# Four PSUM banks for the layers of a gated cross-attention block, with x's transposes in borrowed banks

## The reference

```
n   = layernorm(x)
Q,K,V = n @ Wq.T + bq,  ctx @ Wk.T + bk,  ctx @ Wv.T + bv      # per token: 16 heads x 32
p   = softmax over g of  Q[h] . K[g]                            # within one token, heads against heads
a   = sum over g of p[h,g] * V[g]
x   = x + tanh(g_xattn) * (a @ Wo.T + bo)
out = x + tanh(g_ffn) * (layernorm(x) @ (Wf * scale).T + bf)
```

## Time and profile before

| | us |
|---|---|
| median of 3 runs | 311.43 |
| the profiled execution | 311.65 |
| its span, first to last instruction | 309.9 |
| TensorE matmul busy | 276.1 (89%) |
| VectorE busy | 226.8 (73%) |
| ScalarE busy | 127.8 (41%) |
| GpSimd busy | 119.5 (39%) |

### The profile page before, as it was taken

The page is one execution under the profiler, slowest core; times in us unless marked ns, Lnnn a source line. Parts: engine busy times, 40 slices in busy tenths (PEclk is TensorE's granted clock), DMA queues, the critical chain, the costliest instruction groups (busy, mean ns, idle before and its releaser), DMA issues.

```text
span 309.9 us, 7795 instructions
## 1 busy us (share of the span) xinstructions
PE 276.1 (89%) x3124; PEld 220.8 (71%) x3124; DVE 226.8 (73%) x364; ACT 127.8 (41%) x243; POOL 119.5 (39%) x126
## 2 busy tenths in 40 slices
PE   7989995599794599999989999999996999799696
PEld 6868874477673388787868777777775878686585
DVE  3769999569544499579974897489947694698673
ACT  5554344650536202852168204931286006636310
POOL 3143319712255015831382236531583015211732
PEclk9999999689998989999999999999999999899699
DMA  6938881500407640572226530763037102423002
GB/s 229 391 93 268 181 268 71 112 26 0 137 30 242 139 137 4 169 170 98 104 72 203 130 135 0 262 144 135 0 115 184 43 0 70 106 33 122 17 35 102
DMA packets 57830, 37.03 MB, mean 119 GB/s; under 512 B 35920, under 2 KB 45392, under 8 KB 57808
## 3 DMA queue, kind: packets, MB, share of 16 engines
q1 hardware_dynamic: 57808, 36.73, 39.4%
HBM read 25.71 MB, written 11.01 MB: 118 GB/s over the span
## 4 chain that ended last, share of the span: by engine, by line
DVE 25%; DMA 20%; PE 17%; issue 12%; POOL 9%; ACT 8%; SPq 8%; DVEq 0%; POOLq 0%; ACTq 0%
PE acc L463 11%; DMA v_scratch<-v_or_norm 6%; DMA x_scratch<-raw_spare 4%; DMA out<-late 4%; ACT late L775 4%; DVE stats L914 4%; PE score_ps L463 4%; SPq L362 3%; DMA x_spare<-wf_t 3%; POOL rstd L1266 3%; POOL shift L1271 3%; DVE late L1086 2%; DVE spread L1055 2%; DVE k_t L974 2%; SPq L347 2%
## 5 line engine op out<-in xcount | busy, mean ns | idle before, releaser
L463 PE MATMUL acc<-wo_parts,xa_parts 128*128 128x512 f32 x168 | 46.6, 436 | 9.4 <-ACT xa_parts L692 6.8
L1266 POOL TENSOR_TENSOR rstd<-var_eps,minus_half 128x1 f32<-128x1 f32 (+1 forms) x24 | 21.5, 895 | 83.7 <-DVE var_eps L925 83.7
L463 PEld LDWEIGHTS acc<-wo_parts,xa_parts 128*128 128x128 f32 x168 | 34.7, 211 | 18.7 <-issue 4.6
L463 PE MATMUL acc<-wk_parts,ctx_parts 128*128 128x512 f32 x144 | 38.9, 426 | 6.5 <-DVE late L1086 4.1
L775 ACT ACTIVATE late<-attn_ps 32x256 f32<-32x256 f32 x112 | 42.1, 376 | 2.6
L748 ACT ACTIVATE v_or_norm<-late,shift,rstd 128x512 f32<-128x512 f32 x12 | 9.8, 814 | 76.2 <-POOL shift L1271 76.2
L463 PEld LDWEIGHTS acc<-wk_parts,ctx_parts 128*128 128x128 f32 x144 | 28.8, 206 | 15.7 <-issue 5.7
L463 PE MATMUL acc<-wv_parts,ctx_parts 128*128 128x512 f32 x144 | 34.7, 395 | 0.0
L463 PE MATMUL acc<-wq_parts,xa_parts 128*128 128x512 f32 x144 | 33.9, 391 | 0.1
L463 PE MATMUL acc<-wf_parts,x_parts 128*128 128x512 f32 (+1 forms) x132 | 30.1, 383 | 1.9 <-DVE v_or_norm L967 1.9
L463 PEld LDWEIGHTS acc<-wq_parts,xa_parts 128*128 128x128 f32 x144 | 26.7, 188 | 6.2 <-DVE k_t L974 0.4
(11 more groups left out here) (112 smaller groups left out, 465.6 us busy)
## 6 DMA issues: line engine op xcount, KB each, us to landing
x_norm<-x SPq DMA_DIRECT2D x8, 512.0 KB, 3.9
v_scratch<-v_or_norm SPq DMA_DIRECT2D x8, 512.0 KB, 3.2
v_keys<-v_scratch SPq DMA_DIRECT2D x16, 256.0 KB, 3.7
x_res<-x SPq DMA_DIRECT2D x8, 512.0 KB, 3.3
ctx_raw<-ctx_t SPq DMA_DIRECT2D x7, 512.0 KB, 4.5
out<-late SPq DMA_DIRECT2D x13, 256.0 KB, 2.7
x_scratch<-raw_spare SPq DMA_DIRECT2D x5, 512.0 KB, 3.1
raw_spare<-x_scratch SPq DMA_DIRECT2D x20, 128.0 KB, 2.6
```

Of the source, the lines that this page charges most:

```text
L463: last = pe.matmul(dst, left(a, k), right(b, k), start=(n == 0), stop=(n == len(terms) - 1))
L1266: nc.gpsimd.tensor_tensor(rstd[which][:, t], var_eps[which][:, t], minus_half[:, t], ALU.pow).then_inc(n_rstd[which], count)
```

## The change

`turn_ps` is gone and `acc` has four banks: two sets of two. By the function `bank`, v and k write the second set and q, o and f the first, with exceptions: chunk 0's v is in the attention banks, chunk 2 has k and q exchanged, and o of the last two chunks is in the second set. The transposes of x go into score, attention or layer banks for chunks 0, 1 and 2; those of x2 into the score banks, for chunk 5 into layer banks.

```diff
-        acc = [psum(f"acc{i}") for i in range(2)]
-        turn_ps = [psum(f"turn_ps{i}") for i in range(2)]
+        acc = [psum(f"acc{i}") for i in range(2 * TILES)]
...
+        def bank(layer, c, t):
+            even = acc[t][:], acc[TILES + t][:]
+            if layer == "v":
+                return attn_ps[:, BANK * t:BANK * (t + 1)] if first(c) else even[1]
+            if layer == "k":
+                return even[0 if second(c) else 1]
+            if layer == "q":
+                return even[1 if second(c) else 0]
+            if layer == "o":
+                return even[1 if isinstance(c, int) and c >= CHUNKS - 2 else 0]
+            return even[0]
+        def x1_bank(c, t):
+            return (score_ps[t][:], attn_ps[:, BANK * t:BANK * (t + 1)], acc[TILES + t][:])[c]
+        def x2_bank(c, t):
+            return acc[t][:] if late_f(c) else score_ps[t][:]
```

```diff
             def score(c):
...
+                pe.sem_inc(pe_passed, 1)
+                reached(pe, x2_lo, TILES * (c - 2 if final(c) else c - 1))
```

On SyncE, scale and Wf are issued ahead of `load_x(1)`:

```diff
+            sp.dma_start(scale_row[:], scale.partition_broadcast(P)).then_inc(scale_in, DMA)
+            for j in range(2):
+                load_w(WF, j)
             load_x(1)
...
             load_res(0)
-            sp.dma_start(scale_row[:], scale.partition_broadcast(P)).then_inc(scale_in, DMA)
-            for j in range(2):
-                load_w(WF, j)
```

```diff
+            def q_pads(c):
+                act.wait_ge(q_biased, 1 if first(c) else 2)
...
+                for slot in range(PAD):
+                    nc.scalar.activation(q_pad[:, slot], q_t[:], ACT.Identity, scale=own_slot[:, slot:slot + 1]
+                                         ).then_inc(q_padded, 1)
...
             def q_bias(c):
+                dve.wait_ge(q_turned, TILES * (c + 1))
+                nc.vector.tensor_tensor(q_t[:], q_t[:], bq_heads[:].unsqueeze(3).broadcast_to([P, QH, KC, GT]),
+                                        ALU.add).then_inc(q_biased, 1)
```

TensorE's steps after the change:

```diff
             def tensor_step(i):
...
                 score(i)
                 if final(i):
                     o_layer(i - 1, "v", i, (0,))
                     late_f_tile(i - 2, 0)
                     o_layer(i - 1, "v", i, (1,))
+                    attend(i)
+                    turn_x2(i - 1, (0,))
                     late_f_tile(i - 2, 1)
-                    turn_x2(i - 1, x2_read(i - 2), (0,))
-                    attend(i)
                     return
...
+                o_layer(i - 1)
+                k_layer(i + 1)
+                q_layer(i + 1)
                 attend(i)
+                if late_f(i - 1):
+                    v_layer(i + 1, tiles=(0,))
+                    turn_x2(i - 1)
+                    return v_layer(i + 1, tiles=(1,))
+                turn_x2(i - 1)
+                v_layer(i + 1)
+                f_layer(i - 1)
```

```diff
+            def first_step():
                 scores_turn(0)
                 softmax_a(0)
-                q_turn(1, 0)
                 k_bias(1)
-                q_turn(1, 1)
                 softmax_b(0)
                 spread_first(0)
-                q_bias(1)
+                q_turn(1, 0)
+                q_turn(1, 1)
+                dve.wait_ge(bq_made, PAD)
+                q_pads(1)
+                norm_stats(0, x_norm, 2)
                 v_bias(1, 0)
-                norm_stats(0, x_norm, 2)
                 v_bias(1, 1)
...
             def second_step():
...
                 v_bias(2, 0)
-                turned_lo(x2_parts, x2_hi, x2_lo, 0)
+                norm_stats(0, x_norm, 3)
+                x2_low(0)
                 v_bias(2, 1)
-                norm_stats(0, x_norm, 3)
...
             def vector_step(i):
...
                 o_residual(i - 1, 1)
-                turned_lo(xa_parts, x1_hi, x1_lo, i + 1, src=x1_source(i + 1))
+                x1_low(i + 1)
+                if exists(i + 2):
+                    norm_stats(0, x_norm, i + 2)
+                spread_first(i)
+                second_stats(i - 1, 0)
                 k_turn(i + 1, 0)
-                spread_first(i)
+                second_stats(i - 1, 1)
                 k_turn(i + 1, 1)
-                second_stats(i - 1, 0)
                 k_bias(i + 1)
                 q_turn(i + 1, 0)
-                second_stats(i - 1, 1)
-                if exists(i + 2):
-                    norm_stats(0, x_norm, i + 2)
                 q_turn(i + 1, 1)
-                q_bias(i + 1)
-                turned_lo(x2_parts, x2_hi, x2_lo, i - 1)
+                q_pads(i + 1)
...
+                x2_low(i - 1)
```

More of the change, by code:

```diff
@@ new lines, in _ @@
+            exp(0)
+            w_high(WF, 0)
+            w_high(WF, 1)
+            def first_step():
+                spread_some(0)
+                act.wait_ge(gates_done, 1)
+                act.wait_ge(consts_in, 2 * DMA)
+                for row, n in ((bo_row, 0), (bf_row, 1)):
+                    nc.scalar.activation(row[:], row[:], ACT.Identity, scale=tanh_g[:, n:n + 1]
+                                         ).then_inc(rows_scaled, 1)
+                attn_copy(0, (0,))
+                x1_apply(2)
+                attn_copy(0, (1,))
+                x1_high(2)
+                exp(1)
+                attn_copy(0, (2, 3))
+                attn_high(0, 0)
+                attn_high(0, 1)
@@ L1100, in _ @@
             norm_stats(0, x_norm, 0)
+            for t in range(TILES):
+                k_turn(0, t)
             w_low(WV, 1)
             w_low(WQ, 0)
-            turned_lo(xa_parts, x1_hi, x1_lo, 0)
-            for t in range(TILES):
-                k_turn(0, t)
+            x1_low(0)
             w_low(WQ, 1)
@@ L1359, in pool_step @@
                     spread_last(i)
+                if exists(i + 2) and not first(i - 1):
+                    root(0, i + 2)
                 if exists(i - 1):
@@ L1362, in pool_step @@
                     root(1, i - 1, 1, 1)
-                if exists(i + 2):
-                    root(0, i + 2)
+                if first(i - 1):
+                    root(0, 3)
                 if exists(i - 1):
```

411 lines of the change are left out of this document (186 added, 225 removed).

## The result

The kernel after takes 290.13 us (median of 4 runs, 289.82 to 291.31) beside 312.38 us of the kernel before (4 runs); the ratio is 0.937, with a 95% interval from 0.928 to 0.947. Ratios leave out executions more than 1.5% above the fastest of their kernel, so they are not the quotients of the medians. The forecast was 295 us in a range from 287 to 304: the direction and the range held, and the gain was 5 us larger than forecast.

A forecast was written before the change was run, and what follows sets the result against it. TensorE, busy 276.1 of 309.9 us, was taken as the bound, each part priced by its waits. Gains of 4.9 + 4.5 - 2.5 + 2.0 + 7.5 = 16.4 gave a 293.5 us span, forecast 295 us, range 287 to 304.

The forecast's parts named there:

- head, to the queries of chunk 2: Start to chunk 2's query projection: 8.4 us removed, less 3.2 for GpSimd meetings and 0.3 for scalings, gains 4.9 us.
- second step, to the start of the queries of chunk 3: Up to chunk 3's query projection: banks give 1.9 us and an earlier SyncE chain 2.6, together 4.5 (3 to 6).
- low clock behind its stand: TensorE stands some 5 us before chunk 3's queries and its clock falls: 2.5 us lost, ends 1.5 and 3.4.
- middle, score 3 to score 6: Regular middle steps: feed-forward no longer waits for the value bias; gain 2.0 us, ends 0 and 2.7.
- tail, score 6 to the end: Last steps: new orders cover stands and low clock, 10.5 us in all; gain 7.5, 8.5 at best, 2.4 at worst.
- 0.3 for the scalings: Head: ScalarE's scalings replacing padding for chunks 0 and 2 cost 0.3 us; for chunk 0, 0 to at most 0.8.
- Part 2: Stretch to chunk 3's query projection: key stands go, chunk 0's store is late next; 4.5 us gained, 2.5 lost to clock.
- the 1.9 us go: Middle: TensorE's waits for the value bias, 1.9 us in four steps, vanish as feed-forward leaves the value projection's bank.
- The wait of 1.85 stays in part, about 1.1: Tail: of TensorE's 1.85 us wait about 1.1 stays, as ScalarE has chunk 5's x2 between its copies.
- the first rival: Whole kernel: GpSimd costs VectorE nothing and the clock holds, 288 us; chance 0.22.
- The second rival: Second step: head's time is given back at the store if SyncE's chain starts no earlier, 304 us; chance 0.18.
- The third: Later steps: slower, the store stays late in every step and query projections wait, 325 us; chance 0.05.

The follow-up runs named there:

- a run without that wait: Kernel after with chunk 0's store issued ahead of the load of chunk 2's values: 285.17 us, ratio 0.925.
- the run with both edits: Kernel after with statistics of the next x set back late and keys and queries on exchanged banks from chunk 2 on: 296.75 us, ratio 0.951.
- the run with late statistics: Kernel after with statistics of the next x set back behind those of x2 in the regular steps, as before: 297.26 us, ratio 0.954.

## Why the prediction was right, and what it had too small

The sum of terms, each against its measurement from the marks of the two traces:

| term | forecast | measured |
|---|---|---|
| head, to the queries of chunk 2 | 4.9 | 3.7 (64.14 to 60.46) |
| second step, to the start of the queries of chunk 3 | 4.5 | 4.4 (8.05 less 3.7) |
| low clock behind its stand | -2.5 | -2.1 (score 3 is 5.9 earlier, the queries 8.05) |
| middle, score 3 to score 6 | 2.0 | 4.5 |
| tail, score 6 to the end | 7.5 | 10.0 |
| sum | 16.4 | 20.5 |

**Head.** The mechanism held: no stand before chunk 2's transposes, GpSimd's four weight instructions done at 46.3 us (I had said 46), subtraction at 2.23 us, spreading at 2.58. The meetings took 4.6 us of VectorE's time (1.5 + 1.8 + 1.35 against rows without one), near the upper end of 5.6 that I had drawn, and TensorE stood 1.22 and 2.59 us behind them, 3.8 where I took 3.2. The step that failed is "0.3 for the scalings": score 0 came at 33.56, past the 33 us that I had named as a sign of error, since ScalarE's two scalings (2.17 us) ran until 33.26 and TensorE stood 1.15 us for them, past my bound of 0.8. I had costed the edit by ScalarE's duration alone and had not placed it behind the normalization of chunk 1. Another 0.9 us is most likely not the change's: the keys of chunk 1 start at 25.94 against 25.02 in the kernel before, but at 25.84 in the run with the store first in the kernel before, whose edit acts later. That run reaches the queries of chunk 2 at 65.19; against it the head gave 4.7 us, close to the forecast of 4.9, and that nearness is partly luck, as the scalings and the meetings cost more than I took.

**Second step.** The store was late next, as forecast: VectorE stood 5.35 us for it and TensorE 6.10, and a run without that wait took both away. VectorE's residual came 6.2 us earlier (101.19 against 107.42), of which 3.7 are the head's, so the chain itself gave 2.5 where I had 2.6. Part 2 was right in its mechanism. That its 4.5 meets 4.4 so closely is partly luck: the same code stood 4.99 us in another execution and took 7.21 for the queries.

**Middle.** The failing step is "the 1.9 us go" and "ends 0 and 2.7": I added up listed waits. In three steps 4.5 us came. From the start of the value projection to the next scores, where feed-forward's wait of 0.6 us lay, the kernel before took 11.97 us and the kernel after 11.09: 2.6 us in three steps instead of 1.9. From the output projection to the attention, where the keys are, it took 17.27 and 16.54: 2.2 us, against about 0.1 in my sum. I had seen this part as VectorE's 2.2 us of waiting for the store, but left it out of TensorE's sum, whose list shows 0.24 us for it; the keys' row showed it as duration, 6.05 against 5.60. Before x2's transposes 0.2 us were lost. That the keys' part was the store, through the late statistics, is shown by the run with both edits, in which the pattern comes back; neither of the two edits alone brings it back in the keys.

**Tail.** The failing step is "The wait of 1.85 stays in part, about 1.1", and the 1 us taken off beyond that. All the 10.5 us of the earlier trace rows went but 0.5: the waits left from score 6 on are 0.45, 0.33, 0.30, 0.21 and 0.16 us, and the clock stayed at 1.00. TensorE's timeline where the earlier trace rows had the 1.85:

```profile
253.04 1.19 PE L479 MATMUL acc<-wo_parts,xa_parts 128*128 128x512 f32 x4 [0.45 <-ACT xa_parts L709]
254.56 2.11 PE L479 MATMUL acc<-wo_parts,xa_parts 128*128 128x512 f32 x8 [0.33 <-DVE xa_parts L933]
256.51 2.89 PE L479 MATMUL acc<-wf_parts,x_parts 128*128 128x512 f32 x12
```

Setting back the last attention on TensorE costs 2.7 us of it. How the other 7.3 divide between the output projection ahead of the keys, ScalarE's order and the banks I did not separate.

**Rivals.** The measured 290 us lies nearer to the first rival's 288 than to the forecast's 295. Its reason did not hold, though: GpSimd was not free for VectorE, and the granted clock fell to 0.69 behind the stand at 107. The time came near through the middle and the tail, which gave 5 us more than forecast. What spoke for this rival was misread, too. The pair of subtractions at 35.11 did not slip between GpSimd's instructions: one was under way and ended at 35.75, so only 0.64 us of it were left to meet.

```profile
33.35 2.40 POOL L1277 TENSOR_TENSOR ctx_parts<-ctx_raw,ctx_parts 128x1024 fp32r<-128x1024 f32 x1 [6.27 <-ACT ctx_parts L692]
```

Nor was GpSimd quiet at 171.81: its context split ran until 172.07. Beside an idle GpSimd the pair takes 0.75 us (at 40.48 in the kernel before with the early weight) and not 0.87. The second rival fell: the save began at 84.37 in place of 91.50, so the chain did start earlier. The third did not occur, but the run with late statistics shows that its mechanism is real.

## What to carry to other kernels

In this kernel a wait cost more than its row (0.95 us for a listed 0.71): look for layers whose duration exceeds that of their fellows, and add the lost overlap. When work moves on GpSimd, list VectorE's two-input instructions beside its new place, and put it where VectorE reads PSUM or has nothing to do; the same edit brought no shorter time in the old orders and 4.4 us in the new. When a bank or order removes one wait, ask which transfer on the queue is late next: one store moved ahead of one load gave another 5 us.

## What the runs showed of the hardware

GpSimd and VectorE lengthen each other when both have a row of such instructions: 2.4 us became 3.3 to 3.4 on GpSimd, 1.21 became 3.37 on VectorE. An instruction of VectorE with one of its inputs in PSUM did not: the low part of x took 1.29 us at 33.79 in the kernel after, beside a scaling on GpSimd that ran until 35.10, and 1.25 in the kernel before with GpSimd idle. In the regular steps of the kernel after the two paddings take 4.66 us in place of 2.48 beside GpSimd's residual bias, and TensorE does not stand for them, since the scores that need them come 6.6 us later (213.54 + 4.66 = 218.2, score 6 at 224.82). A granted clock of 0.69, between the levels of 1.2 and 2.4 GHz, followed the stand of 6.10 us (107 to 116 us), and 0.76 one of 1.93 us in the kernel with both edits (170 to 177 us). A longer stand is not always followed by a lower clock: after 2.76 us in the kernel with late statistics and 2.12 in the one with both edits the granted clock was 1.00 (2.4 GHz), and the rows took 5.78 and 6.03 us.
